# Where q and k are normalised, when the squares are made, and when the feed-forward's rows are turned back

## What is computed

```python
for i in range(6):
    x = attn_layer(shift_tokens(x), Wqkv[i], q_scale[i], k_scale[i], Wo[i]) + x
    x = ffn_layer(shift_tokens(x), ln_g[i], ln_b[i], W1[i], b1[i], W2[i], b2[i]) + x

def attn_layer(x, Wqkv, qs, ksc, Wo):       # 16 heads of 64, windows of 32
    q, k, v = split(x @ Wqkv)
    q = l2norm(q) * qs                      # t / max(norm(t), 1e-12)
    k = l2norm(k) * ksc
    q = q * cos * scale + rotate_half(q) * sin * scale
    k = k * cos / scale + rotate_half(k) * sin / scale
    return softmax(masked q k^T * 8 over own and previous window) @ v @ Wo

def ffn_layer(x, g, bln, W1, b1, W2, b2):   # 341 hidden
    xn = layer_norm(x) * g + bln
    a, gate = split(xn @ W1 + b1)
    return a * gelu(gate) @ W2 + b2
```

## Time and profile before

| | us |
|---|---|
| median of three runs | 4828.77 |
| lowest and highest run | 4828.52, 4838.41 |
| the profiled execution | 4834.84 |
| its span, first to last instruction | 4832.9 |
| local phase, first to last scores (in the span) | 492 to 3673 |

### The profile page before, as it was taken

The page is one execution under the profiler, slowest core; times in us unless marked ns, Lnnn a source line. Parts: engine busy times, 40 slices in busy tenths (PEclk is TensorE's granted clock), DMA queues, the critical chain, the costliest instruction groups (busy, mean ns, idle before and its releaser), DMA issues. The chain is left out here.

```text
span 4832.9 us, 167342 instructions
## 1 busy us (share of the span) xinstructions
PE 4224.5 (87%) x70890; PEld 3379.5 (70%) x70890; DVE 3624.7 (75%) x5894; ACT 2545.3 (53%) x3896; POOL 2849.5 (59%) x2141
## 2 busy tenths in 40 slices
PE   6997899999999999999999999999997749658667
PEld 5885677777777777777777777777775439548447
DVE  4445888888888888888888888888885564564554
ACT  2232456655566556565556565566654317546435
POOL 2223777777777777777777777777772037516025
PEclk9776999999999999999999999999998869868878
DMA  0001222232222322222222222222221021222022
GB/s 25 0 0 39 75 63 63 69 79 69 63 70 62 85 62 70 64 80 67 67 67 80 68 63 70 63 68 67 67 66 37 0 59 50 68 61 61 7 63 74
DMA packets 214198, 281.51 MB, mean 58 GB/s; under 512 B 58878, under 2 KB 103716, under 8 KB 212740
## 3 DMA queue, kind: packets, MB, share of 16 engines
q1 hardware_dynamic: 203972, 251.85, 20.1%
q0 software_dynamic: 9536, 19.55, 1.4%
HBM read 54.88 MB, written 18.28 MB: 15 GB/s over the span
## 5 line engine op out<-in xcount | busy, mean ns | idle before, releaser
L1526 POOL TENSOR_TENSOR local_rot<-local_rot,local_sines 128x512 f32<-128x512 f32 x768 | 955.2, 1278 | 825.1 <-DVE local_sines L1605 825.1
L1534 POOL TENSOR_TENSOR local_inv_norm<-local_norm2c,minus_half 128x16 f32<-128x16 f32 x384 | 1126.9, 2935 | 32.0
L1413 ACT COPY local_v_tile<-local_bank 128x1024 f32<-128x1024 f32 x192 | 195.0, 1016 | 713.0 <-PE local_bank L1186 702.6
L1184 PE MATMUL local_bank<-local_wqkv_hi,local_ys_hi 128*128 128x512 f32 x1152 | 491.3, 426 | 23.6 <-POOL local_ys_lo L1517 10.4
L1262 PE MATMUL local_bank<-ident,local_normed 128*128 128x128 f32 x3072 | 405.4, 275 | 91.0 <-DVE local_sines L1605 80.6
L1595 DVE TENSOR_TENSOR local_normed<-local_rot,local_inv_norm 128x1024 f32<-128x1024 f32 x384 | 455.3, 1218 | 32.9 <-issue 26.4
L1605 DVE TENSOR_TENSOR local_rot<-local_bank,local_table 128x1024 f32<-128x1024 f32 x384 | 467.7, 1218 | 7.0 <-issue 7.0
L1605 DVE TENSOR_TENSOR local_sines<-local_bank,local_table 128x1024 f32<-128x1024 f32 x384 | 467.3, 1217 | 0.0
L1610 DVE TENSOR_REDUCE local_norm<-local_squares 128x16 f32<-128x1024 f32 x384 | 464.7, 1211 | 0.0
L1186 PE MATMUL local_bank<-local_wqkv_hi,local_ys_lo 128*128 128x512 f32 x1152 | 453.8, 394 | 0.0
L1185 PE MATMUL local_bank<-local_wqkv_lo,local_ys_hi 128*128 128x512 f32 x1152 | 453.3, 394 | 0.0
(11 more groups left out here) (420 smaller groups left out, 9118.5 us busy)
## 6 DMA issues: line engine op xcount, KB each, us to landing
local_vals<-local_v_tile SPq DMA_DIRECT2D x1152, 130.0 KB
local_vals<-local_v_tile SPq DMA_DIRECT2D x672, 65.0 KB
local_stage<-in_L_ffn_Wqkv SPq DMA_DIRECT2D x6, 1536.0 KB, 8.0
moe_w<-y_rows SPq DMA_DIRECT2D x32, 256.0 KB, 5.1
moe_w<-in_L_ffn_W SPq DMA_DIRECT2D x3, 2048.0 KB, 9.9
x_rows<-moe_rows SPq DMA_DIRECT2D x12, 512.0 KB, 3.8
local_wo<-in_L_ffn_Wo SPq DMA_DIRECT2D x6, 512.0 KB
moe_taken<-x_rows,moe_take POOLq DMA_INDIRECT x149, 2.5
```

The source lines that it names most:

```text
L1184: nc.tensor.matmul(out, hi, wqkv_hi[:, d0:d1], start=True, stop=False)
L1526: last = nc.gpsimd.tensor_tensor(of_heads(rot, a)[:, :, to], of_heads(rot, a)[:, :, to], of_heads(sines, a)[:, :, of], ALU.add)
L1534: nc.gpsimd.tensor_tensor(inv_norm[:, cols], norm2c[:, cols], g.minus_half[:, cols], ALU.pow).then_inc(q["inv_norms_ready"], 1)
```

## The change

The normalisation of q and k leaves VectorE. `rotate` on GpSimd now writes its sums into `normed` and waits for the transposes of the tile before to have read it; a new `normalise` on GpSimd multiplies `normed` in place with the inverse norms. The power of the norms leaves GpSimd: `guard_norms` bounds both norms in one instruction, and ScalarE takes the logarithm and the exponential of minus half of it (a new `invert_norms`, at the head of its iteration); the table load behind the gelus names a set for both functions, and one more load of it stands ahead of the loop. ScalarE also makes the squares of q ahead of the exponentials instead of behind them. `ffn_back` moves from the end of the iteration with t = 2 to that with t = 3, behind the scores, and `scale_norm` moves with it; the projection of k into bank 6 waits for `xn_ready` there.

```diff
@@ TensorE @@
+                        if k % TILES == 3 and is_seq(k // TILES - 1):
+                            pe.wait_ge(q["xn_ready"], seq("xn_ready", k // TILES - 1))
...
                 def ffn_back(n, k):
-                    after_qk(k)
+                    after_qk(k - 1)
...
                         make_scores(k)
+                    if t == 3 and is_seq(n - 1):
+                        ffn_back(n - 1, k)
                     if is_tile(k + 1):
                         project_v(k + 1, k)
...
-                    if t == 2 and is_seq(n - 1):
-                        ffn_back(n - 1, k)
@@ ScalarE @@
+                def invert_norms(m):
+                    act.wait_ge(q["norms_guarded"], tile("norms_guarded", m))
+                    nc.scalar.activation(log_norm[:], norm2c[:], ACT.Ln).then_inc(q["logs_ready"], 1)
+                    act.wait_ge(q["logs_ready"], tile("logs_ready", m))
+                    act.wait_ge(q["qk_normed"], tile("qk_normed", m - 1))
+                    nc.scalar.activation(inv_norm[:], log_norm[:], ACT.Exp, scale=-0.5).then_inc(q["inv_norms_ready"], 1)
...
-                    nc.scalar.activation(table_pick[:, 2:3], table_pick[:, 0:1], ACT.Exp)
+                    nc.scalar.preload_act_table_set("natural_log_exp_and_others")
...
                     if is_tile(k + 1):
+                        invert_norms(k + 1)
                         copy_v(k + 1)
+                    if t == 3 and is_seq(n - 1):
+                        scale_norm(n - 1)
+                    if is_tile(k + 2):
+                        square(k + 2, 0)
                     if is_tile(k):
                         exponentials(k)
-                    if is_tile(k + 2):
-                        square(k + 2, 0)
...
                         ffn_normalise(n - 1)
-                        scale_norm(n - 1)
@@ GpSimd @@
                 def rotate(m, a):
                     pool.wait_ge(q["products_ready"], tile("products_ready", m, a + 1))
+                    pool.wait_ge(q["qk_turned"], tile("qk_turned", m - 1, a + 1))
...
-                        last = nc.gpsimd.tensor_tensor(of_heads(rot, a)[:, :, to], of_heads(rot, a)[:, :, to], of_heads(sines, a)[:, :, of], ALU.add)
+                        last = nc.gpsimd.tensor_tensor(of_heads(normed, a)[:, :, to], of_heads(rot, a)[:, :, to], of_heads(sines, a)[:, :, of], ALU.add)
...
-                    nc.gpsimd.tensor_tensor(inv_norm[:, cols], norm2c[:, cols], g.minus_half[:, cols], ALU.pow).then_inc(q["inv_norms_ready"], 1)
+                def guard_norms(m):
+                    pool.wait_ge(q["norms_ready"], tile("norms_ready", m))
+                    nc.gpsimd.tensor_scalar(norm2c[:], norm2[:], 1e-24, None, ALU.max).then_inc(q["norms_guarded"], 1)
+
+                def normalise(m, a):
+                    pool.wait_ge(q["rotated"], tile("rotated", m, a + 1))
+                    pool.wait_ge(q["inv_norms_ready"], tile("inv_norms_ready", m))
+                    nc.gpsimd.tensor_tensor(of_heads(normed, a), of_heads(normed, a), inv_norm[:, a * HEADS:(a + 1) * HEADS].unsqueeze(2).to_broadcast([P, HEADS, HD]),
+                                            ALU.mult).then_inc(q["qk_normed"], 1)
@@ VectorE @@
-                    nc.vector.tensor_tensor(of_heads(normed, a), of_heads(rot, a), inv_norm[:, a * HEADS:(a + 1) * HEADS].unsqueeze(2).to_broadcast([P, HEADS, HD]),
-                                            ALU.mult).then_inc(q["qk_normed"], 1)
...
-                    dve.wait_ge(q["qk_normed"], tile("qk_normed", m - 1, a + 1))
+                    dve.wait_ge(q["rotated"], tile("rotated", m - 1, a + 1))
...
+                    dve.wait_ge(q["norms_guarded"], tile("norms_guarded", m - 1))
```

31 lines of the change are left out of this document (12 added, 19 removed).

## The result

The changed kernel takes 4791.4 us (median of four runs, 4780.73 to 4791.83), the kernel before 4829.24 beside it: a ratio of 0.9912, 95% interval 0.9894 to 0.993. The forecast was 4710, a gain of 119 us; 38 came. The profiled execution is 4791.83 us long.

The account below looks back on a forecast made before the run. TensorE, busy 95% of the local phase, was taken as the bound, with only its waiting removable. 154 + 10 less 50 us of new waits, plus 5 for an earlier start, gave 119 off 4828.8: 4710 us, range 4655 to 4795.

Parts of the forecast that it names:

- The upper bound: Most that TensorE's removed waits and refills could give: 154 us in the local phase, 164 with the changes of layer.
- both waits: TensorE's waits for the product with the sines (76.1 us) and for turning back y_hat (39.0 us), both to go.
- The small waits for ScalarE's copies: New TensorE waits because ScalarE's chain to the copied q has no slack: 0.15 us a tile, 0.6 per sequence.
- Normalise fits on GpSimd: GpSimd's two multiplications per tile, taken at 2.09 us each, would stay hidden up to 2.65 us each.
- the first division's: New wait from t = 2 into t = 3: VectorE's first division releases the scores 0.2 us late.
- that for the exponentials in t = 3: New wait in t = 3: ScalarE's square starts later, so the exponentials release the turned probabilities 0.25 us late.
- a sign of failure: The prediction would be wrong if ScalarE stood waiting for the bounded norms once the values are projected.
- rival E: No gain, TensorE's waits only change their name: 4825 to 4832 us, needing 3.3 us of new waits per sequence; chance 0.06.
- the changes of layer: At five places the projection waits for VectorE's split of the weights; about 10 us more may go.
- Rival D: Slower: VectorE locks GpSimd out, so each normalise lasts 3.3 to 4.5 us; near 4890 us, chance 0.07.
- The earlier start of 5 us: The local phase starts some 5 us sooner, since the first tiles have two powers fewer on GpSimd.
- B: Dearer new waits, from ScalarE's five-step chain or a normalise of 3.2 us: 4765 us taken, chance 0.20.

Follow-up runs that it names:

- e8: Changed kernel with 64 small matmuls and their 64 weight loads issued once ahead of TensorE's first scores; 4784.28 us, 0.9901 of the kernel before.
- e9: Changed kernel with the mask's two matmuls ahead of the scores issued four times over at t = 3; 4808.48 us, 0.9946 of the kernel before.
- e10: Changed kernel without the scores of every second chunk, so its output is another; 4612.19 us, 0.9541 of the kernel before.
- e5: Changed kernel with GpSimd's normalise waiting, at the five changes of layer, for VectorE's first two weight splits; 4883.53 us on another chip, 0.987 of the kernel before.
- e4: Changed kernel with 128 no-operations ahead of the local loop, absent from the trace, so read as a second run of it; 4898.46 us on another chip, ratio 0.9908.
- e6: Changed kernel with values projected ahead of the scores at t = 3 and VectorE's output addition ahead of the first division at t = 2; 4851.15 us, another chip, ratio 0.9815.
- e3: Changed kernel with the normalise of q and k put back on VectorE, all else as changed; 4797.34 us, 0.992 of the kernel before.
- e7: Changed kernel with the edits of e5 and e6 together; 4724.17 us, 0.978 of the kernel before.

## Why the prediction was wrong

**What held.** The upper bound was read rightly: both waits are gone, and with them the time for refilling. Turning q and k takes 1.87 us from start to start (median), where it took 2.25. The small waits for ScalarE's copies are there, too short to be listed: turning the probabilities takes 0.93 in place of 0.87 and the first half of the values 0.88 in place of 0.79, the 0.15 of the forecast. Normalise fits on GpSimd, even cheaper than I took it, and the small logarithm and exponential on ScalarE were near 0.2 us. Rows of the changed kernel by line (times, busy us, mean ns, idle before them), to be held against the earlier trace rows:

```profile
L1551 POOL TENSOR_TENSOR local_normed<-local_normed,local_inv_norm 128x1024 f32<-128x1024 f32 x384 | 732.8, 1929 | 276.1 <-ACT local_inv_norm L1441 276.1
...
L1438 ACT ACTIVATE local_log_norm<-local_norm2c 128x32 f32<-128x32 f32 x191 | 44.4, 233 | 143.9 <-POOL local_norm2c L1546 143.4
L1441 ACT ACTIVATE local_inv_norm<-local_log_norm 128x32 f32<-128x32 f32 x191 | 43.8, 229 | 6.1
```

1929 ns against my 2090. The Trainium skill, GPSIMD Engine Reference, section Performance versus the Vector engine, led to an estimate of 2.25 us, above both. Of the new waits the first division's is there, 11.1 us in 28 times, 0.4 each where I took 0.2; that for the exponentials in t = 3 came as 0.06, where I took 0.25. ScalarE stands 143.4 us waiting for the bounded norms. I had named this as a sign of failure if it happens once the values are projected; it happens before, since the copy of the values behind it still waits 548.0 us for their projection.

**What failed, first: the sum itself.** It ran "upper bound less new waits", and each new wait was one for another engine. It put at nothing, without a reason, that TensorE also needs its instructions, though the same view that gave had 23 us of stalls that no engine ended. Taking waits out packs TensorE's stream, and where 128 instructions of the values and 260 of the scores now follow each other, the feeding of the stream is the next limit. That took 43.9 + 20.6 + 4.1 + 0.9 = 69.5 us, where it was 23.4: 46 us of the gain. The places of the stalls in the packets, e8, e9 and e10 show the cause. The sum also took "the work of TensorE itself" for unchanged: seven of the stalls in tiles with t = 3 brought the low clock with them, 1.2 us each, another 8 us. My rival E had the form of this (new waits of 3.3 us per sequence in place of the old) but I looked for them among the engines.

**Second: the changes of layer.** I booked 10 us of gain there. Rival D had the right mechanism, the contention between VectorE's two-operand split and GpSimd, and the row that showed it, and I priced only GpSimd's side of it, in the ordinary tiles, where it doesn't occur. What counts is VectorE's split, with TensorE 3.10 us behind it and then at the low clock. The pair of tiles rose from 36.87 to 38.44 us, 8 us over five changes of layer where 10 less were booked: 18 in all, and five times the 3.66 that e5 gives back are 18 too.

**Third, small:** tiles with t = 2 take 14.00 and not 13.7, in part by the division's wait: 0.3 x 43 = 13 us. Of the phase's 114 us forecast 31 came; 46 + 8 + 18 + 13 = 85 stand against the missing 83, as near as terms of this size can be told. The earlier start of 5 us came as 6, but e4, the same program, starts its scores at 488.4 in place of 486.0, so that this says little.

The time lies inside the range of 4655 to 4795 all the same, near its upper end, and that was luck: B, the rival that made the range reach so far, came out in size without its cause, since no chain of ScalarE and no slow normalise made it.

## What to carry to other kernels

When a change takes waits away from an engine that issues many short instructions, count its instructions against its time in the stretch that gets packed: here 256 instructions came at best every 3.3 us, and stretches of 390 in that time stalled. Look in the trace of before for idle time with no releaser in the midst of one line; here it grew from 31 to 87 us when the waits went, and a few long instructions moved into the dense stretch were worth more than a second engine relieved (e6 against e3, 52 us against 14; 47 against 13 on their own chips). Look at the granted clock behind each long pause of TensorE, too: busy time that grows while the work stays the same is the sign. A long instruction moved to GpSimd has to be held against every two-operand SBUF instruction of VectorE that it may newly meet, also one that comes only once per layer.

## What the runs showed of the hardware

- TensorE's instructions come in packets of 16384 bytes, 250 to 252 matmuls and weight loads each (e10 and the changed kernel), 256 with the semaphore instructions. The closest starts of two packets are 3.3 us apart, a packet takes 1.04 us (median), and the first instruction after a stall starts 1.41 us (median) behind its packet's end. What asks for the next packet, and when, stays open.
- The place of such stalls hangs on the count of all instructions ahead of them: 128 more at the start moved the stalls by four tiles (e8). The phase was 10 us shorter with it, where two runs of one program differ by 5.
- Beside GpSimd's multiplication, VectorE's split with two SBUF inputs took 2.92 us, without it 1.21; the multiplication beside it took up to 2.88, otherwise 1.90.
- TensorE's clock fell after pauses: after all five of some 3.1 us at changes of layer, and after eight of the stalls for instructions, of 1.75 to 2.40 us (thirteen times in the changed kernel, once in the one before, never in e7's phase). At the layer change with k = 94 it was idle for 3.10 us, ran three matmuls at 0.95, and from 2041.10 to 2042.50 the granted clock is 0.50, the lower of its two levels (1.2 GHz), where its rows of 512 columns take 0.63 us instead of 0.39. The windows view of the changed kernel, ahead of the pause, and behind it:

```profile
2020.00:2037.00 17.00, 16.49 (x338) 12.35 (x336) 12.87 (x27) 10.38 (x14) 8.76 (x8) 1.00 0.25 66
2040.30:2041.10 0.80, 0.77 (x3) 0.67 (x4) 0.80 (x1) 0.00 (x0) 0.80 (x1) 0.95 0.89 195
2041.10:2042.50 1.40, 1.40 (x5) 0.96 (x4) 1.40 (x1) 0.00 (x0) 0.89 (x1) 0.50 0.61 190
```

Over the phase the granted clock is 0.99 where it was 1.00. That looks like little, but thirteen stretches at half the clock, 44 us together, are up to 22 us of lost work by an estimate from these rows, and TensorE's busy time is 24 us longer than before.
